# A chain of cross-attention layers on one core: the first projections with gamma products between the gate inputs, batch 0 ahead of batch 1

## The reference

```python
x_norm = _rms(x, norm1_scale)
z = x_norm @ Wz + bz
k = x_norm @ Wk + bk
gamma_base = sigmoid(gelu(z @ Wg1 + bg1) @ Wg2 + bg2)
gamma_mod  = sigmoid(gelu(k @ Wgc1 + bgc1) @ Wgc2 + bgc2)
gamma = clip(gamma_base * gamma_mod, 1e-6, 1 - 1e-6)
def step(h_prev, zt_gt):
    z_t, g_t = zt_gt
    gate = sigmoid(z_t @ Wgz + bgz + h_prev @ Wgh + bgh)
    h_t = (1.0 - gate) * h_prev + gate * z_t + g_t * h_prev
    return (h_t, h_t)
```

## Time and profile before

| | us |
|---|---|
| median of 3 runs | 912.06 |
| lowest, highest | 911.32, 912.16 |
| the profiled execution | 911.81 |
| its span in the trace | 909.6 |
| TensorE busy | 836.3 (92%) |
| VectorE busy | 517.2 (57%) |
| ScalarE busy | 449.9 (49%) |
| mean granted clock of TensorE | 0.977 |

### The profile page before, as it was taken

How to read it: one execution, slowest core, us unless ns; L and a number is a source line. 1 busy time by engine, 2 the same in 40 slices (tenths; PEclk the granted TensorE clock), 3 DMA queues, 4 the chain that set the end, 5 groups by cost and what they waited for, 6 DMA issues and landing times.

```text
span 909.6 us, 10241 instructions
## 1 busy us (share of the span) xinstructions
PE 836.3 (92%) x4229; PEld 382.9 (42%) x4232; DVE 517.2 (57%) x714; ACT 449.9 (49%) x662; POOL 48.5 (5%) x41
## 2 busy tenths in 40 slices
PE   5998999989899999987998998999888989888987
PEld 2544444444344445452324244234355434544342
DVE  3368999843431032167636035479679495994442
ACT  3586322554434225252442723667865468752634
POOL 1000000020000000012200000000021000210000
PEclk9999999999999999988899999999989999999999
DMA  7000000011000000030000000000000000000011
GB/s 291 1 1 1 0 0 1 15 79 47 2 0 1 0 1 0 1 138 0 1 1 1 1 0 1 1 0 0 1 1 1 1 0 1 1 1 1 1 47 47
DMA packets 3004, 15.60 MB, mean 17 GB/s; under 512 B 656, under 2 KB 912, under 8 KB 2320
## 3 DMA queue, kind: packets, MB, share of 16 engines
q1 hardware_dynamic: 2816, 12.88, 3.8%
q0 software_dynamic: 144, 2.10, 0.5%
HBM read 12.87 MB, written 2.10 MB: 16 GB/s over the span
## 4 chain that ended last, share of the span: by engine, by line
PE 72%; ACT 15%; DVE 10%; DMA 2%; issue 1%; SPq 0%; POOL 0%; DVEq 0%; ACTq 0%
PE ps L421 70%; DVE VB L669 3%; ACT AR L653 3%; DMA WA<-in_m 2%; ACT AR L1923 2%; ACT AR L1913 1%; DVE AR L2236 1%; ACT AR L1607 1%; DVE AR L685 1%; ACT AR L1889 1%; ACT AR L658 1%; ACT AR L656 1%; DVE AR L511 1%; ACT AR L1906 1%; ACT AR L1919 1%
## 5 line engine op out<-in xcount | busy, mean ns | idle before, releaser
L421 PE MATMUL ps<-AR,WA 128*128 128x512 f32 (+2 forms) x716 | 310.9, 599 | 8.1 <-DVE AR L2469 3.6
L421 PEld LDWEIGHTS ps<-AR,WA 128*128 128x128 f32 (+2 forms) x716 | 131.7, 190 | 174.9 <-issue 159.1
L421 PE MATMUL ps<-AR 128*64 128x128 f32 (+5 forms) x680 | 100.6, 424 | 8.7 <-ACT AR L1923 2.0
L421 PE MATMUL ps<-AR,CN 128*128 128x512 f32 (+3 forms) x304 | 102.8, 599 | 4.8 <-DVE AR L514 1.9
L421 PEld LDWEIGHTS ps<-AR 128*64 128x64 f32 (+4 forms) x680 | 53.3, 166 | 48.2 <-issue 22.4
L685 DVE TENSOR_TENSOR AR<-ps,AR 128x512 f32<-128x512 f32 x24 | 16.6, 692 | 99.4 <-ACT AR L658 99.4
L653 ACT ACTIVATE AR<-ps 77x2048 f32<-77x2048 f32 x24 | 43.9, 1868 | 42.3 <-PE ps L421 31.1
L669 DVE TENSOR_REDUCE VB<-ps 128x16 f32<-128x1232 f32 x32 | 44.9, 1438 | 29.4 <-PE ps L421 28.6
L421 PEld LDWEIGHTS ps<-AR,CN 128*128 128x128 f32 (+2 forms) x304 | 35.2, 157 | 52.2 <-issue 35.0
L421 PE MATMUL ps<-KB,WA 128*128 128x512 f32 (+1 forms) x120 | 53.0, 609 | 0.9 <-ACT AR L1906 0.9
L2366 DVE SCALAR_TENSOR_TENSOR AR<-AR,VC 128x512 f32<-128x512 f32 x72 | 50.6, 748 | 5.4 <-ACT AR L1847 4.4
(11 more groups left out here) (334 smaller groups left out, 1124.7 us busy)
## 6 DMA issues: line engine op xcount, KB each, us to landing
WA<-in_m SPq DMA_DIRECT2D x1, 2856.0 KB, 9.6
WA<-in_m SPq DMA_DIRECT2D x1, 2560.0 KB, 15.8
X<-in_xT POOLq DMA_DIRECT2D x1, 2048.0 KB, 9.5
WA<-in_m SPq DMA_DIRECT2D x1, 2048.0 KB, 8.4
out<-X SPq DMA_DIRECT2D x4, 512.0 KB, 3.1
WB<-in_m SPq DMA_DIRECT2D x1, 1024.0 KB, 4.8
AR<-in_rows SPq DMA_DIRECT2D x1, 640.0 KB, 10.2
WA<-in_m SPq DMA_DIRECT2D x1, 512.0 KB, 16.6
```

The costliest lines, as they stand in the source:

```text
L421: return nc.tensor.matmul(out, lhsT, rhs, start=first, stop=last)
```

## The change

On TensorE the gate inputs and the gamma products of a block are issued in the order gate(0,0), gate(0,1), gamma(0,0), gate(1,0), gamma(0,1), gate(1,1), gamma(1,0), gamma(1,1), where the numbers are batch and mo. A gamma(b, mo) is the product of the lower 64 rows into bank 3 and that of the upper 64 rows into bank 1; both mo use the same two banks, and gamma(b, 1) waits until ScalarE has read both gammas of gamma(b, 0). In block 1 the z products wait for the eviction of block 0's gate inputs too.

On ScalarE the bf16 copy of z of batch 0 comes between the z evictions of the two batches. The gate sigmoids and gammas are done for batch 0 and then for batch 1. The copy of 1 + gamma of block 0 into OPG is done behind the loop, in place.

On VectorE the gamma work, the products and the scans are done for batch 0 and then for batch 1, and the clip of block 0's gamma writes into OPG instead of GB.

```diff
--- before.py
+++ after.py
@@ -862,6 +862,7 @@  (TensorE)
                 for b in BS:
                     if j:
+                        pe.wait_ge(*after("zg", 2 * b + 2))
                         pe.wait_ge(*after("gam", 4 * (b + 1)))
@@ -898,20 +899,31 @@  (TensorE)
-                for b in BS:
+                def gate_input(b, mo):
+
                     pe.wait_ge(*after("z", nk(j, 4, 2 * b + 1)))
                     if not j:
                         pe.wait_ge(*after("norm_ln", NORMS["r1"] + B * J))
-                    for mo in range(DC):
-                        for c in range(DC):
-                            last = mm(bank(b, 2 * mo), feat(w("Wgz", 2), c, mo), Z[:, c, b, tj(j)], c == 0, c == DC - 1)
-                        last.then_inc(sem("zg_mm"), 1)
-                for b in BS:
+                    for c in range(DC):
+                        last = mm(bank(b, 2 * mo), feat(w("Wgz", 2), c, mo), Z[:, c, b, tj(j)], c == 0, c == DC - 1)
+                    last.then_inc(sem("zg_mm"), 1)
+
+                def gamma(b, mo):
+
                     pe.wait_ge(*after("gg", n2(j, b)))
-                    for k, (lo, mo, to) in enumerate(((0, 0, 3), (0, 1, 1), (64, 0, 0), (64, 1, 2))):
-                        if k == 2:
-                            pe.wait_ge(*after("zg", nk(j, 4, 2 * b + 1)))
+                    if mo:
+                        pe.wait_ge(*after("gam", nk(j, 8, 4 * b + 1)))
+                    for lo, to in ((0, 3), (64, 1)):
                         mm(bank(b, to), WA[lo:lo + 64, mats["Wg2c"][1] + mo * P:mats["Wg2c"][1] + (mo + 1) * P], GG[b][lo:lo + 64, :]).then_inc(sem("gam_mm"), 1)
+
+                gate_input(0, 0)
+                gate_input(0, 1)
+                gamma(0, 0)
+                gate_input(1, 0)
+                gamma(0, 1)
+                gate_input(1, 1)
+                gamma(1, 0)
+                gamma(1, 1)
@@ -1578,33 +1590,37 @@  (ScalarE)
+            def narrowed(j, b):
+
+                act.wait_ge(*after("z", nk(j, 4, 2 * b + 1)))
+                nc.scalar.activation(Z16[:, :, b, tj(j)], Z[:, :, b, tj(j)], ACT.Copy).then_inc(sem("z16"), 1)
+
             for j in range(J):
                 for b in BS:
                     for mo in range(DC):
                         ...
+                    if b == 0:
+                        narrowed(j, b)
                 ...
-                for b in BS:
-                    act.wait_ge(*after("z", nk(j, 4, 2 * b + 1)))
-                    nc.scalar.activation(Z16[:, :, b, tj(j)], Z[:, :, b, tj(j)], ACT.Copy).then_inc(sem("z16"), 1)
-                if j:
-                    for b in BS:
-                        act.wait_ge(*after("gclip", b + 1))
-                        nc.scalar.activation(OPG[:, :, b, tj(0)], GB[b], ACT.Identity, bias=cn("ones")[:, 0:1]).then_inc(sem("opg"), 1)
-                    act.wait_ge(*after("opg", B))
+                narrowed(j, 1)
                 act.wait_ge(*after("h", 8 + j * 4))
                 for b in BS:
                     for mo in range(DC):
                         act.wait_ge(*after("zg", nk(j, 4, 2 * b + mo)))
                         nc.scalar.activation(U0[b][:, mo, :], ZG[:, mo, b, tj(j)], ACT.Sigmoid).then_inc(sem("g"), 1)
-                for b in BS:
-                    for k, (dst, bias, to) in enumerate(((GB[b][:, 0], v("bg2", 0), 3), (GB[b][:, 1], v("bg2", 1), 1),
-                                                         (SQ[b][:, 0], v("bgc2", 0), 0), (SQ[b][:, 1], v("bgc2", 1), 2))):
-                        act.wait_ge(*after("gam_mm", nk(j, 8, 4 * b + k)))
-                        nc.scalar.activation(dst, bank(b, to), ACT.Sigmoid, bias=bias).then_inc(sem("gam"), 1)
+                    if j:
+                        act.wait_ge(*after("gclip", b + 1))
+                    for mo in range(DC):
+                        for k, (dst, bias, to) in enumerate(((GB[b], "bg2", 3), (SQ[b], "bgc2", 1))):
+                            act.wait_ge(*after("gam_mm", nk(j, 8, 4 * b + 2 * mo + k)))
+                            nc.scalar.activation(dst[:, mo], bank(b, to), ACT.Sigmoid, bias=v(bias, mo)).then_inc(sem("gam"), 1)
+            for b in BS:
+                act.wait_ge(*after("gclip", b + 1))
+                nc.scalar.activation(OPG[:, :, b, tj(0)], OPG[:, :, b, tj(0)], ACT.Identity, bias=cn("ones")[:, 0:1]).then_inc(sem("opg"), 1)
@@ -2043,7 +2058,7 @@  (VectorE)
                 for b in BS if j == 0 else ():
-                    TS(GB[b], GB[b], LO, HI, ALU.max, ALU.min).then_inc(sem("gclip"), 1)
+                    TS(OPG[:, :, b, tj(0)], GB[b], LO, HI, ALU.max, ALU.min).then_inc(sem("gclip"), 1)
```

## The result

The changed kernel takes 915.86 us in the median of 8 executions (913.37 to 918.2) against 911.31 for the kernel before (8 executions, 906.12 to 912.4). The ratio is 1.0066, 95% interval 1.0048 to 1.0084: slower, by 4.55 us between the medians and 6.0 by the ratio (4.4 to 7.7). Forecast were 916.0 and a range of 913.9 to 918.2.

The account below looks back on a forecast made before the run. TensorE, busy 92% of the span, bounds the kernel; three branches with little slack meet at about 90 us. A last gamma 3.9 us later gives 911.81 + 3.9 = 915.7, set 0.25 higher against the runs' median: 916.0, range 913.9 to 918.2.

Parts of the forecast that it names:

- Pairing saves nothing: TensorE's eight 64-row gamma products already run two at a time, so pairing them gains no time there.
- A pair in between costs 1.25 us, the last gate input comes 2.5 later: TensorE, block 0: each gamma pair between gate inputs costs 0.86 + 2 x 0.20; two move the last gate result to 47.3.
- The unknown half of the shape change: TensorE's way back from 64 to 128 rows: an extra between 0 and 0.09 us, taken as 0.09.
- the drain: Changing TensorE's tiling mode drains the engine; priced at 0.20 from the trace, read literally 0.07 more per change, 916.7 in all.
- The wait for two emptied banks: Block 0: TensorE stands still from 48.3 to 49.94 ahead of gamma(1,1); block 1's z products start 2.4 us later.
- Block 1: Last gate eviction done at 71.77, then sigmoid, gammas, last product pair, gammas: last gamma at 76.05, 3.9 us later.
- ScalarE's removals bring nothing: One narrowing (0.95) and two OPG copies (2.18) removed ahead of the table load gain nothing, since ScalarE then waits for TensorE.
- the slack of 2.3: First sweep's second gate was done 2.3 us before VectorE used it; with the copies moved, VectorE's 82.19 becomes 86.0.
- VectorE's order: Batch 0's scans ending earlier helps nobody, as the sweep's second half waits for all scans; scans end 1.6 us later.
- already costs that 1.7 us: TensorE's clock fall over 73.2 to 77.0 before; the gaps near 72 to 76 replace its gap, so nothing is added.
- rival A: TensorE's clock falls in the new stall at 48.3, losing 1.7 us in the z products: 917.7; chance 0.13.
- The marks in the timeline: Signs of being right: last gamma at 76.05, first sweep's gates at 84.9, long TensorE stretch from 107.1 instead of 103.23.

Follow-up runs that it names:

- E4: E1 with TensorE's order of before (all gate inputs, then all gamma products); ratio 1.0007 to the kernel before.
- E1: The changed kernel with four gamma banks, gamma(b,1) going to banks 0 and 2; ratio 1.0000 to the kernel before.
- E6: The kernel before with TensorE's new gate input and gamma order alone and four banks; ratio 1.0062.
- E0: The changed kernel run again without any edit; ratio 1.0041, 914.64 against 910.11 us for the kernel before.
- E3: The kernel before with ScalarE's moves alone: batch 0's narrowing and the OPG copies placed as changed, clip into OPG; ratio 1.0009.
- E7: The kernel before with VectorE's order alone (gamma work, products and scans batch by batch); ratio 1.0002.
- E9: The kernel before with its 2.7 us TensorE gap ahead of the first sweep filled by two unused 64-row products; ratio 0.9995.
- E5: E1 with TensorE doing batch 0's gate inputs and gammas, then batch 1's, OPG copies back ahead of the table load; ratio 1.0015 to the kernel before.
- E8: The changed kernel with unused 64-row products in both blocks' stalls ahead of gamma(1,1) and one behind the last; ratio 1.0034 to the kernel before.

## Why the prediction was right, point by point

- *Pairing saves nothing.* Right: the loads came two at a time before, and a pair of products takes the same passes after.
- *A pair in between costs 1.25 us, the last gate input comes 2.5 later.* Right: 7.66 against 5.15, undone in E4. The unknown half of the shape change is 0.10, where 0.09 was taken. The prediction read the drain of the Trainium skill, "TensorEngine Tiling (Array Packing)", Key Properties, literally as 0.07 more a change; this is not borne out, four changes cost 0.79.
- *The wait for two emptied banks.* Right in place and size: z products at 11.44 against 8.95, +2.5 for a forecast of +2.4, and E1 takes 1.8 of it away. The split of it was wrong. The prediction gave 1.0 to shape changes and 1.4 to the longer stall; measured, the 2.5 are the later last gate input (1.72 passes of two pairs, 0.79 shape changes), and from there the z products wait as long as before (3.78 against 3.80). What the two banks cost is that ScalarE's batch order does not shorten this wait to the 1.96 of E1. And E6 shows that without ScalarE's batch order the same stall arises with four banks, from the old wait ahead of the z products.
- *Block 1.* Right: without a fall of the clock (E0) the last gamma is 4.0 us later, forecast 3.9.
- *ScalarE's removals bring nothing, its OPG copies use up the slack of 2.3.* Right: E3 is equal, and in the changed kernel VectorE's sweep starts 3.9 us late in E0 (46.48 against 42.57), forecast 3.8.
- *VectorE's order.* Right: E7.
- *A fall of the clock that "already costs that 1.7 us" near 72 to 76.* Wrong: in the profile of before it cost 0.2 us, since VectorE's branch ends that close behind (E9). In E0 and the changed kernel no fall came there, and one came later.
- *The clock, rival A.* In the profiled execution it happened: 915.57 us with the fall at 50 us, and 5.7 us at the long stretch. I had it at 0.13, arguing from one gap of 1.82 us without a fall. It does happen behind 1.7 us, in the profiles of the changed kernel and E6, and not in E0; and the gap of before behind which the prediction read one had none behind it in E7. Of the eight executions, four with a mean clock of 0.978 or 0.979 have spans of 911.2 to 913.8, four with 0.974 have 914.0 to 915.9. Where those of the changed kernel fell was seen in the one profile alone.
- *The number.* The mechanism gives a difference, 3.9 us; measured are 3.7 to 4.55, and 6.0 by the ratio of the first comparison. That 916.0 lies within 0.2 us of 915.86 is in part luck: the forecast stood on 912.06, the median of three, where the eight executions of before have 911.31. From there the sum gives 915.2; that falls of the clock in the changed kernel's executions (mean clock 0.974 to 0.979, in E0 0.978 to 0.985) make the rest is likely and not shown.
- *The marks in the timeline.* The last gamma (76.05 forecast, 76.31 measured), the gates (84.9, 85.08) and the long stretch (107.1, 107.37) agree partly by luck: the execution reached its first gate eviction 1.55 us earlier, and lost 1.7 to the fall at 50 us. Against the first gate eviction they are 1.7 to 1.8 later than forecast, nearly all of it this fall.
- *Not tested.* That a larger cut of VectorE's and TensorE's branch together would gain is left open; each alone gains nothing that the times can show. Nor were two gamma banks tried with another order of TensorE.

## What to carry to other kernels

Ask of every reordering what each engine's queue has behind the new wait. Here gammas ahead of the last gate input delayed it by 2.5 us a block. The batch order could have won most of this back, but two PSUM banks given up kept TensorE waiting for ScalarE, 3.2 us over two blocks, while a saving of 3 us on ScalarE lay ahead of a point that another engine sets. Where three branches meet with slacks of 0.2 to 2.3 us, shortening one (E3, E5, E7, E9) is worth about 0.2 us at most in the traces and lengthening one costs all of it but its slack.

## What the runs showed of the hardware that I had not expected

- A fall of TensorE's clock to its lower level (1.2 GHz) came in different places in executions of one program, behind a stall of 1.7 us in one (0.74 and 0.83 over 48 to 56) and not in another (1.00, E0). Behind the same gap of 2.7 us it came in the profile of before (0.55 over 73.2 to 77) and not in E7 (1.00 over 72 to 76).
- It also came with no gap just ahead of it: over 84 to 88 us in the changed kernel and E8, behind products of 1 and 4 columns, with TensorE recorded as busy for the whole window (4.00 of 4.00). A filled gap is then no guarantee. The same products ran in E0 with the clock at 1.00 over 84 to 88, so what brings the fall stays open.
- Part of the spread between executions of one kernel goes with the clock. Of the 31 of before beside E0, those with a mean clock of 0.985 have a median span of 905.4 us and those with 0.979 one of 910.1.
- The shape change between 128 and 64 rows costs 0.20 us each way (0.79 for four, E4).
